# An accumulator output that nobody reads, on VectorE's block scale operations of x and h

## The reference

```python
BLOCK = 16
def fp4_quant_dequant(x):
    xb = x.reshape(shape[:-1] + (shape[-1] // BLOCK, BLOCK))
    scale = jnp.max(jnp.abs(xb), axis=-1, keepdims=True) / 6.0
    scale = jnp.maximum(scale, jnp.float32(1e-12))
    xn = xb / scale
    idx = jnp.searchsorted(_MID, jnp.abs(xn))
    q = _GRID[idx] * jnp.sign(xn) * scale
    return q.reshape(shape)
...
Q = _xpos(X @ W_Q); K = _xpos(X @ W_K, downscale=True); V = X @ W_V
p_attn = jax.nn.softmax(Q K^T, axis=-1) * D       # D = 0.9 ** |n - m|
x = _layernorm(x + p_attn @ V)
h = jax.nn.silu(fp4_linear(x, w_gate)) * fp4_linear(x, w_up)      # 256 -> 704
x = _layernorm(x + fp4_linear(h, w_down))                         # 704 -> 256
```

## Time and profile before

| | |
|---|---|
| median of 3 runs | 1103.22 us (1102.05 to 1105.62) |
| the profiled execution | 1102.92 us, its span 1101.0 us |
| mean granted TensorE clock | 0.977 of full speed |
| TensorE busy | 996.8 us, 91% |
| VectorE busy | 901.7 us, 82% |
| GpSimd busy | 829.0 us, 75% |
| ScalarE busy | 636.2 us, 58% |
| chain that ended last | GpSimd 29%, VectorE 29%, issue 26%, TensorE 8%, ScalarE 4%, transfers 2% |

### The profile page before, as it was taken

One profiled execution on the slowest core, in us unless ns is written; L12 is line 12 of the kernel. 1 busy time (PEld: TensorE's weight loads), 2 busy tenths in 40 slices (PEclk: granted clock), 3 DMA queues, 4 the chain that ended last, 5 costly groups with the idle time before them and its releaser, 6 DMA issues.

```text
span 1101.0 us, 20402 instructions
## 1 busy us (share of the span) xinstructions
PE 996.8 (91%) x6002; PEld 879.3 (80%) x6002; DVE 901.7 (82%) x1874; ACT 636.2 (58%) x1575; POOL 829.0 (75%) x1034
## 2 busy tenths in 40 slices
PE   8989999999999999999999999999999997778755
PEld 7778888888788888888788888788888886667655
DVE  7878889888888898888888898888888886676554
ACT  3636666566566665665666665665666555453422
POOL 6968787887888788787888788787978785564423
PEclk9999999999999999999999999999999998898988
DMA  7123243233423234243423234243433222221100
GB/s 284 44 88 117 80 139 115 78 120 114 141 85 122 88 112 139 67 135 101 140 92 120 89 103 143 80 132 95 131 94 127 90 77 82 72 73 63 44 10 15
DMA packets 116111, 111.26 MB, mean 101 GB/s; under 512 B 12576, under 2 KB 93728, under 8 KB 114080
## 3 DMA queue, kind: packets, MB, share of 16 engines
q1 hardware_dynamic: 115312, 108.91, 30.9%
q10 hardware_dynamic: 688, 1.05, 0.3%
HBM read 69.53 MB, written 40.37 MB: 100 GB/s over the span
## 4 chain that ended last, share of the span: by engine, by line
POOL 29%; DVE 29%; issue 26%; PE 8%; ACT 4%; DMA 2%; SPq 1%; POOLq 0%; DVEq 0%; ACTq 0%
POOL prob L2314 5%; POOL rot_a L2212 5%; POOL h L2199 4%; DVE rot_b L1606 3%; DVE rot_a L1606 3%; POOL xv L2199 3%; DVE turned L1701 2%; DVE hsc L1623 2%; DVE hsc L1618 2%; POOL xt_l L2228 2%; POOL rs L2273 2%; DVE h L1669 2%; POOL h_last L2205 2%; DVE xv L1717 2%; DVE xv L1724 2%
## 5 line engine op out<-in xcount | busy, mean ns | idle before, releaser
L2199 POOL TENSOR_TENSOR h<-h,hsc 128x704 f32<-128x704 f32 x126 | 168.5, 1337 | 57.8 <-DVE h L1675 34.5
L607 PE MATMUL ps_oy<-v_h,pt_h 128*128 128x256 f32 x512 | 152.9, 299 | 38.0 <-POOL pt_l L2286 37.5
L2314 POOL TENSOR_TENSOR prob<-prob,decay_t 128x512 f32<-128x512 f32 x128 | 164.7, 1294 | 0.0
L607 PE MATMUL ps_g<-wgu_h,xqt_h 128*128 128x480 f32 (+1 forms) x380 | 150.6, 396 | 8.9 <-DVE h L1643 5.3
L609 PE MATMUL ps_oy<-v_h,pt_l 128*128 128x256 f32 x512 | 147.5, 288 | 0.0
L608 PE MATMUL ps_oy<-v_l,pt_h 128*128 128x256 f32 x512 | 147.3, 288 | 0.0
L609 PE MATMUL ps_g<-wgu_h,xqt_l 128*128 128x480 f32 (+1 forms) x380 | 142.8, 376 | 0.0
L608 PE MATMUL ps_g<-wgu_l,xqt_h 128*128 128x480 f32 (+1 forms) x380 | 142.7, 376 | 0.0
L607 PEld LDWEIGHTS ps_oy<-v_h,pt_h 128*128 128x128 f32 x512 | 99.7, 195 | 50.0 <-POOL pt_l L2286 45.0
L1168 ACT ACTIVATE ps_oy<-xv 128x256 f32<-128x256 f32 x63 | 24.5, 389 | 166.7 <-DVE r L1762 149.9
L1682 DVE TENSOR_TENSOR ht_l<-ps_t,ht_h 128x512 fp32r<-128x512 f32 x126 | 56.4, 485 | 62.3 <-ACT ht_h L1257 62.3
(11 more groups left out here) (274 smaller groups left out, 3237.7 us busy)
## 6 DMA issues: line engine op xcount, KB each, us to landing
parking<-turned SPq DMA_DIRECT2D x122, 256.0 KB, 2.0
landing<-parking SPq DMA_DIRECT2D x488, 64.0 KB, 2.0
rope_t<-rope SPq DMA_DIRECT2D x15, 1024.0 KB, 5.6
xres<-x SPq DMA_DIRECT2D x64, 128.0 KB, 2.1
out<-yout SPq DMA_DIRECT2D x63, 128.0 KB, 2.0
xin<-x_t SPq DMA_DIRECT2D x14, 512.0 KB, 4.2
first_rope<-rope SPq DMA_DIRECT2D x2, 512.0 KB, 8.1
decay_t<-decay SPq DMA_DIRECT2D x1, 960.0 KB, 12.0
```

The lines of the kernel that those rows point to most:

```text
L607: pe.matmul(dst, a_h, b_h, start=(start and i == 0), stop=False)
L2199: return tt(blocks(dst), blocks(src), sc[:, which, at:at + n].unsqueeze(2).to_broadcast([P, n, QB]), ALU.mult)
L2314: tt(prob[:, keys], prob[:, keys], decay_t[:, lo:lo + CW], ALU.mult).then_inc(decayed, 1)
```

## The change

The `tensor_scalar` that makes the block scales of x and of h gets a second output, its accumulator, of one column. Column 0 of a new tensor takes it for h, column 1 for x. Nothing reads that tensor. Order, semaphores and the other operations stay as they are. The helper is also called for the last tile's two parts of h.

```diff
+        unread = sb("unread", [P, 2])
...
-            def block_scales(sc, done):
+            def block_scales(sc, done, which=0):
 
                 nc.vector.tensor_scalar(sc[:, 0, :], sc[:, 2, :], TIES_DOWN / 6.0, MIN_SCALE * TIES_DOWN, ALU.mult,
-                                        ALU.max).then_inc(done, 1)
+                                        ALU.max, accum_out=unread[:, which:which + 1]).then_inc(done, 1)
...
-                    block_scales(xsc, xscale_done)
+                    block_scales(xsc, xscale_done, 1)
```

## The result

The changed kernel takes 1085.34 us, the median of 3 runs (1082.87 to 1087.01), against 1103.22 (1102.05 to 1105.62): a ratio of 0.9833, 95% interval 0.9802 to 0.9864. It is 17.9 us faster in the medians, 17.5 in the spans (1101.0 to 1083.5), at the same mean granted clock (0.976 after, 0.977 before). The forecast was 14.1 us of gain, 1089; the time lies in the range, near its lower end, and the gain is a little above the 17.3 us that the prediction had worked out for an accumulator that costs nothing. In gain the interval of the ratio is 15.0 to 21.8 us, so the change gave a little more than forecast.

A forecast was written before the change was run, and what follows sets the result against it. TensorE was taken as nearest bound, on a path VectorE, GpSimd, TensorE late by VectorE's queue. Six blocks 12.6, first steps 1.7, last block 0.25, closing chain -0.4: 14.1 us gained, 1089 us; range 1084.5 to 1098.

The forecast's parts named there:

- step 2: Third step of each eight-step block: h form's queue time falls from 0.87 to 0.16 us; gain 0.6 us.
- step 4: Fifth step of a block: h stall of 0.97 us goes, TensorE's waits for x and landed low part shrink; gain 0.55.
- Step 6: Seventh step of a block: as the third, but a cast's end caps it at 0.57 us; gain 0.5.
- Steps 0 and 3: First and fourth steps of a block: limited by TensorE's projection and its 0.26 us wait respectively; gain 0.25 us each.
- steps 1 and 5: Second and sixth steps of a block: TensorE doesn't wait and GpSimd's queue sets the x product; no gain.
- step 7: Last step of a block: VectorE's idle time covers the x form, h's 0.1 us matches its wait; loss 0.05.
- The last block: Final steps: x stall covered by VectorE's 3.30 us idle for TensorE; only 0.25 us gained, for the block's first step.
- closing chain: Behind the last block: four changed operations that don't wait now; loss 0.4 us.
- rival 1: Accumulator is dear, 0.2 to 0.35 us of VectorE's queue: 1093 us at 0.2, 1100 at 0.35; chance 0.12.
- rival 2: TensorE waits anew for landing transfers or GpSimd; with half the gain lost 7 us, 1096; chance 0.06.
- rival 3: Stalls stay and each changed operation costs 0.1 us more: 6 to 7 us slower, 1109; chance 0.05.
- rival 4: Stalls go but the accumulator write-out eats them, at 0.35 us or more: 1100 to 1104; chance 0.07.

The follow-up runs named there:

- e11: Kernel before, no accumulators, last block issuing `landed_low` between the two decays and ScalarE's cast for it ahead of those of h: 1093.30 us, ratio 0.9918.
- e10: Changed kernel, last block issuing `landed_low` between the two decays and ScalarE's cast for it ahead of those of h: 1074.17 us, ratio 0.9741.
- e8_r1_first: Changed kernel with GpSimd's `r2_variance` and `r2_inverse` moved behind `landed_low` in steps 0, 2, 4 and 6: 1086.74 us, ratio 0.9852.

## Why the prediction was right, point by point

**The mechanism.** The whole wait went, as taken. Of the two VectorE forms compared in one kernel, it is the plain SBUF-to-SBUF `tensor_scalar` on columns in a row that waits for GpSimd's running operation. The longest times are 172 and 199 ns after; the half-length operations show the dependence on GpSimd's end, and the padded pattern shows that the accumulator isn't needed for it. The prediction had taken the quick form for the one that waits, which fits all of these runs, and hadn't seen that a pattern does as much.

**The step that was mis-sized** is the queue cost of an accumulating operation, taken as 0.1 us on top of the plain 0.06. (The prediction says 0.1 "in all", but its sum adds it to the 0.06.) It measures 0.08 to 0.09 us in all, where the plain form held the queue 0.06 to 0.07 us for h and 0.07 to 0.08 for x when it didn't wait. So it costs 0.01 to 0.02 us more than plain, which is below the low end (0.06) of that term too: the read starts together with the next operation and holds nothing. With it the even steps come out as the prediction's own working gives them: step 2 saves 0.87 - 0.09 = 0.78, less 0.01 for x, 0.77, and gained 0.70; step 4 gained 0.72. The Trainium skill's fixed cost of some 150 cycles ("VectorE: DVE Perf Modes", "The TRN2 errata"), by which the write-out would be 0.16 us as an estimate, isn't what these rows show of the queue: four pairs in 0.31 us. The row of the accumulating operation itself is of that length (154 to 199 ns); the next operation starts before it ends, after 0.08 to 0.09 us.

**Step 6** was capped at 0.57 by a cast that ends late. Its usual gain is 0.71, so the cast moves too in four blocks of six. In the other two (steps 38 and 54) VectorE stands 0.37 and 0.38 us for it and the gain is 0.32 and 0.31: the cap is real where the landing transfer comes late, and lower than 0.57.

**Steps 0 and 3** gained 0.19 and 0.16 for 0.25 each, steps 1 and 5 lost 0.03, step 7 gained 0.02 for a loss of 0.05. These are as argued: TensorE's projection, the small wait, and GpSimd's queue set them. In step 0 the 1.07 us of the x form became 0.59 us of idleness ahead of `rot_mul`, against none in the earlier trace rows:

```profile
502.63 0.16 DVE L1624 TENSOR_SCALAR_CACHE_REDUCE xsc<-xsc 128x16 f32<-128x16 f32 x1
...
507.24 1.23 DVE L1607 TENSOR_TENSOR rot_a<-ps_g,rope_t 128x1024 f32<-128x1024 f32 x1 [0.59 <-issue]
```

**The sum.** Up to the x scale operation of step 56 the changed kernel is 16.06 us ahead (887.12 to 871.06). 0.2 of it is there at the first x scale operation (59.92 to 59.7) and has nothing to do with the change; the first steps gained 2.2 (predicted 1.7), and the six blocks 13.7 (predicted 12.6), which is 6 x 2.44 = 14.6 less the 1.1 that steps 38, 52 and 54 give back, to within 0.2.

**The last block** is covered, as predicted. Steps 59 and 61 lost x stalls of 1.27 and 1.24 us and kept their lengths (17.76 to 17.67, 17.51 to 17.53). In step 61 VectorE's idleness ahead of the residual grew from 3.17 to 4.24; first before, then after:

```profile
973.20 1.24 DVE L1623 TENSOR_SCALAR xsc<-xsc 128x16 f32<-128x16 f32 x1
...
979.62 0.42 DVE L1762 TENSOR_TENSOR r<-ps_oy,x 128x256 f32<-128x256 f32 x1 [3.17 <-PE ps_oy L795]
```

```profile
957.53 0.16 DVE L1624 TENSOR_SCALAR_CACHE_REDUCE xsc<-xsc 128x16 f32<-128x16 f32 x1
...
963.98 0.42 DVE L1763 TENSOR_TENSOR r<-ps_oy,x 128x256 f32<-128x256 f32 x1 [4.24 <-PE ps_oy L796]
```

The step of the earlier trace rows, step 60, can't be compared so: it went from 17.54 to 18.91 us, at a lower granted clock. As in the earlier trace rows, before and after:

```profile
955.66:973.20 17.54, 14.32 (x79) 12.71 (x79) 12.66 (x28) 8.61 (x24) 9.68 (x15) 0.90 0.23 76
938.62:957.53 18.91, 15.53 (x79) 13.91 (x79) 11.81 (x30) 8.75 (x24) 9.84 (x15) 0.82 0.22 70
```

Step 62 has it the other way round, 18.78 us at 0.82 before and 17.68 at 0.90 after. The stretches at the lower of the two levels (1.2 GHz) fall on other steps now, and over the whole stretch from step 56 to the end the clock is 0.89 in both.

From the start of step 56 to the end 1.4 us more were gained, where the prediction had -0.15 (0.25 less 0.4). Of the closing chain, taken as -0.4, the traces show next to nothing: from the last h scale operation to the end it is 27.8 us after (1083.5 - 1055.72) and 28.0 before (1101.0 - 1073.01), and the three scale operations in it start their reciprocals 0.24, 0.22 and 0.22 us later, against 0.22, 0.22 and 0.21. The other 1.2 us lie in steps 56 to 65, above all step 58 (20.06 to 19.32) and step 65 (16.33 to 15.86). They are hardly the change's: the kernel with the one-column writes, which has the long waits still, takes 212.25 us from step 56 to its end, the changed one 212.44 and the kernel before 213.88. So some 1.4 of the 17.5 us are more likely luck of the two profiled executions. The six blocks had luck against them: between `e11` and `e10`, which part in the accumulators alone, the change gives 15.7 us in the six blocks and nothing from step 56 on (-0.4), 17.8 in all. No run holds the clock still, so what moves the steps of the last block stays open.

**The rivals.** The dear accumulator (rival 1) is out: 0.08 us a pair. The handed-on gain (rival 2) is real but small, 1.1 us in steps 38, 52 and 54; it comes in full when GpSimd's order is pushed further, as `e8_r1_first` shows. The form that waits on (rival 3) needed the h operation of step 2 to end where GpSimd's does; it ends 0.76 us before (535.00 against 535.76). No change (rival 4) is out with rival 1.

## What to carry to other kernels

If a short VectorE operation from SBUF to SBUF takes some 0.15 us at best and over 1 us at worst, put its row beside GpSimd's: if it ends where GpSimd's operation does, take it out of the quick form, by an accumulator output or by a pattern such as the eleven groups of four here, and cost that at 0.01 to 0.02 us of queue. Its worth is not the sum of the stalls but, step by step, the lesser of the stall and of what the bound engine waits behind it; here the eight kinds of step gave 0 to 0.7 us for stalls of up to 1.1, and two stalls in one queue were worth more together than one by one in two steps of the start. Then look where the bound engine's largest wait is: an order of two operations in the last block gave 9 to 11 us more.

## What the runs showed of the hardware that was not expected

- The accumulator's read is a row of its own of 80 to 86 ns, but the next operation starts with it (534.93 both). VectorE's accumulator costs far less than ScalarE's rows of 208 ns would suggest.
- A one-column write of 0.06 us adds at most some 0.02 us to the queue, since its row lies inside the next operation's.
- A `tensor_scalar` on 44 elements takes 136 ns at best and 1128 at worst on columns in a row, 148 and 199 on the eleven groups of four. At this size the form in a row saves 0.01 us and risks a whole GpSimd operation.
- The plain form gets in between two GpSimd operations that follow each other without a gap: it ends at 542.59, when the first half has ended (542.54 to 542.58) and the second runs.
